# First context tile of a cross-attention kernel in two transfers, with its rounding residues and Gram matrix ordered ahead of the bias rows

## The reference

```
q, k = Wq y + bq, Wk y + bk            (per batch: 128 x 1024)
v    = Wv x + bv
scores = q k^T / sqrt(128)             (within each head: 16 x 16)
out  = softmax(scores) v
o    = Wo out + bo + x
result = (o - mean(o)) / sqrt(var(o) + 1e-5) * gn_w + gn_b    (mean, var over the batch)
```

## Time and profile before

| | us |
|---|---|
| median of 3 executions | 166.63 |
| lowest and highest | 166.38, 167.06 |
| the profiled execution, its own time | 166.47 |
| its span (first to last instruction) | 164.6 |
| PE busy in it | 154.2 (94%) |
| DVE busy | 149.5 (91%) |
| ACT busy | 137.2 (83%) |
| POOL busy | 98.0 (60%) |
| DMA queue of SP, share of 16 engines | 83.3% |

### The profile page before, as it was taken

One profiled execution on the slowest core, in us unless ns is written; L12 is line 12 of the kernel. 1 busy time (PEld: TensorE's weight loads), 2 busy tenths in 40 slices (PEclk: granted clock), 3 DMA queues, 4 the chain that ended last, 5 costly groups with the idle time before them and its releaser, 6 DMA issues. The chain is left out here.

```text
span 164.6 us, 3752 instructions
## 1 busy us (share of the span) xinstructions
PE 154.2 (94%) x932; PEld 121.0 (74%) x932; DVE 149.5 (91%) x686; ACT 137.2 (83%) x354; POOL 98.0 (60%) x162
## 2 busy tenths in 40 slices
PE   7998999999999999999999999999999999998820
PEld 7896887777777788887777777888777777785500
DVE  1788999999999999999999999999999999987861
ACT  3685499999999999999999999999999999767351
POOL 3039267776666676667766666766777666541120
PEclk9999999999999999999999999999999999999995
DMA  5999859999999999998999999999999977631136
GB/s 188 403 407 412 313 196 330 324 338 296 350 342 348 346 357 396 345 336 272 380 377 354 336 344 351 358 334 339 329 374 338 377 308 263 255 127 59 75 127 255
DMA packets 14277, 50.84 MB, mean 309 GB/s; under 512 B 1712, under 2 KB 1712, under 8 KB 14256
## 3 DMA queue, kind: packets, MB, share of 16 engines
q1 hardware_dynamic: 13824, 50.08, 83.3%
q10 hardware_dynamic: 432, 0.53, 0.9%
HBM read 33.82 MB, written 16.78 MB: 307 GB/s over the span
## 5 line engine op out<-in xcount | busy, mean ns | idle before, releaser
L751 PE MATMUL o_ps<-x_sb,m_sb 128*128 128x512 f32 x124 | 61.1, 612 | 0.7 <-ACT out_sb L404 0.7
L751 PE MATMUL g_ps<-hl_sb 128*128 128x258 f32 x256 | 47.0, 308 | 0.0
L484 DVE TENSOR_TENSOR hl_sb<-y_sb,hl_sb 128x512 fp32r<-128x512 f32 x64 | 43.7, 687 | 0.0
L574 DVE BATCH_NORM_STATS2 bn<-o_ps 128x6 f32<-128x512 f32 x62 | 40.3, 685 | 1.4 <-PE o_ps L751 1.4
L325 ACT CAST hl_sb<-y_sb 128x512 fp32r<-128x512 f32 x64 | 39.2, 618 | 1.9 <-DMA y_sb<-in_ctx_dram 1.9
L404 ACT ACTIVATE out_sb<-o_ps,shift,gain 128x1024 f32<-128x1024 f32 x31 | 37.4, 1206 | 2.6
L252 POOL TENSOR_TENSOR lsuma<-hl_sb 128x256 f32<-128x256 f32 x30 | 21.9, 729 | 25.9 <-DVE hl_sb L484 25.9
L751 PEld LDWEIGHTS g_ps<-hl_sb 128*128 128x128 f32 x256 | 35.5, 194 | 0.2 <-DVE hl_sb L484 0.2
L263 POOL TENSOR_TENSOR lsumb<-hl_sb 128x256 f32<-128x256 f32 x30 | 21.9, 729 | 17.5 <-DVE hl_sb L484 17.5
L751 PEld LDWEIGHTS o_ps<-x_sb,m_sb 128*128 128x128 f32 x124 | 21.0, 191 | 14.7 <-issue 14.7
L274 POOL TENSOR_TENSOR lsum<-lsuma,lsumb 128x256 f32<-128x256 f32 x30 | 22.3, 743 | 4.2 <-issue 0.4
(11 more groups left out here) (76 smaller groups left out, 288.9 us busy)
## 6 DMA issues: line engine op xcount, KB each, us to landing
y_sb<-in_ctx_dram SPq DMA_DIRECT2D x32, 512.0 KB, 6.3
x_sb<-in_x_dram SPq DMA_DIRECT2D x32, 512.0 KB, 7.1
out_dram<-out_sb SPq DMA_DIRECT2D x31, 512.0 KB, 6.3
w_in<-in_weights_dram ACTq DMA_DIRECT2D x1, 256.0 KB, 5.4
out_dram<-out_sb ACTq DMA_DIRECT2D x1, 256.0 KB, 2.6
out_dram<-out_sb SPq DMA_DIRECT2D x1, 256.0 KB, 2.8
cols<-in_columns_dram ACTq DMA_DIRECT2D x1, 3.0 KB, 3.4
```

The source lines that it names most:

```text
L484: nc.vector.tensor_tensor(hl_sb[:, b % SLOTS, chunks, C:2 * C], y_sb[:, b % SLOTS, chunks, :], hl_sb[:, b % SLOTS, chunks, 0:C].bitcast(F3 ...
L574: nc.vector.bn_stats(bn[:, b % 2, half, :], o_half(b, half)).then_inc(bn_done, 1)
L751: return nc.tensor.matmul(dst, lhsT, rhs, start=start, stop=stop, **more)
```

## The change

The load of context tile 0 becomes two transfers, one of its first four chunks (signalled by a new semaphore `y_first`) and one of the other four (`y_in[0]`); `round_half(0, 0)` and `round_half(0, 1)` wait for one each. DVE takes both residues of batch 0 before the diagonals. PE takes the Gram matrix of batch 0 before the product that makes the bias rows. ACT's `bias_rows` moves behind `round_half(1, 0)` and `copy_cross(0)`. On DVE `scale_wq` moves behind `rest_half(1, 0)` and `mask_and_bias` behind `rest_half(1, 1)`. What is computed stays the same, and so does the number of instructions, but for one more transfer.

```diff
--- before.py
+++ after.py
@@ -106,6 +106,7 @@
 
 
         y_in = [sem(f"y_in{k}") for k in range(SLOTS)]
+        y_first = sem("y_first")
         x_in = [sem(f"x_in{k}") for k in range(SLOTS)]
         out_done = [sem(f"out_done{k}") for k in range(SLOTS)]
         w_loaded = sem("w_loaded")
@@ -189,6 +190,12 @@
                 if b >= SLOTS:
 
                     sp.wait_ge(l_ready, 2 * (b - SLOTS + 1))
+                tile_y = yT[bass.ds(b, 1)].rearrange("a (p j) c -> p (a j c)", p=P)
+                if b == 0:
+
+                    sp.dma_start(y_sb[:, 0, 0:HCH, :].rearrange("p j c -> p (j c)"), tile_y[:, 0:HCH * C]).then_inc(y_first, 16)
+                    sp.dma_start(y_sb[:, 0, HCH:CH, :].rearrange("p j c -> p (j c)"), tile_y[:, HCH * C:CH * C]).then_inc(y_in[0], 16)
+                    return
                 sp.dma_start(y_sb[:, b % SLOTS, :, :].rearrange("p j c -> p (j c)"),
                              yT[bass.ds(b, 1)].rearrange("a (p j) c -> p (a j c)", p=P)).then_inc(y_in[b % SLOTS], 16)
 
@@ -316,7 +323,12 @@
             def round_half(b, half):
                 if not live(b):
                     return
-                if half == 0:
+                if b == 0:
+                    if half == 0:
+                        act.wait_ge(y_first, 16)
+                    else:
+                        act.wait_ge(y_in[0], 16)
+                elif half == 0:
                     act.wait_ge(y_in[b % SLOTS], loads(b))
                     if b >= SLOTS:
 
@@ -406,9 +418,9 @@
 
             round_half(0, 0)
             round_half(0, 1)
-            bias_rows()
             round_half(1, 0)
             copy_cross(0)
+            bias_rows()
             round_half(1, 1)
             round_half(2, 0)
             round_half(2, 1)
@@ -471,11 +483,6 @@
             dve.wait_ge(const_pool, 6)
             nc.vector.tensor_copy(ident_r[:, :], ident[:, 0:P]).then_inc(const_dve, 1)
 
-            dve.wait_ge(c_loaded, 16)
-            nc.vector.tensor_scalar(diag[:, 0, :], ident[:, 0:P], bq_raw, SCALE * E, ALU.mult, ALU.mult).then_inc(const_dve, 1)
-            nc.vector.tensor_scalar(diag[:, 1, :], ident[:, 0:P], bk_raw, -float(E), ALU.mult, ALU.mult).then_inc(const_dve, 1)
-            nc.vector.tensor_scalar(bq_col[:, :], bq_raw, -SCALE * L, None, ALU.mult).then_inc(const_dve, 1)
-
             def rest_half(b, half):
                 if not live(b):
                     return
@@ -483,6 +490,12 @@
                 dve.wait_ge(h_ready, 2 * b + 1 + half)
                 nc.vector.tensor_tensor(hl_sb[:, b % SLOTS, chunks, C:2 * C], y_sb[:, b % SLOTS, chunks, :],
                                         hl_sb[:, b % SLOTS, chunks, 0:C].bitcast(F32), ALU.subtract).then_inc(l_ready, 1)
+
+            def bias_diagonals():
+                dve.wait_ge(c_loaded, 16)
+                nc.vector.tensor_scalar(diag[:, 0, :], ident[:, 0:P], bq_raw, SCALE * E, ALU.mult, ALU.mult).then_inc(const_dve, 1)
+                nc.vector.tensor_scalar(diag[:, 1, :], ident[:, 0:P], bk_raw, -float(E), ALU.mult, ALU.mult).then_inc(const_dve, 1)
+                nc.vector.tensor_scalar(bq_col[:, :], bq_raw, -SCALE * L, None, ALU.mult).then_inc(const_dve, 1)
 
             def scale_wq():
                 dve.wait_ge(w_loaded, 16)
@@ -644,12 +657,13 @@
 
             rest_half(0, 0)
             rest_half(0, 1)
+            bias_diagonals()
+            rest_half(1, 0)
             scale_wq()
-            mask_and_bias()
-            rest_half(1, 0)
             add_gram(0)
             copy_high_sum(0)
             rest_half(1, 1)
+            mask_and_bias()
             copy_sum(0)
             add_query_bias(0)
             rest_half(2, 0)
@@ -854,12 +868,13 @@
             pe.wait_ge(const_dve, 1)
             keep_busy(WARM_UP)
 
+            pe.wait_ge(const_dve, 4)
+            gram(0, 0)
+            gram(0, 1)
+
             pe.wait_ge(const_dve, 6)
             product(row_ps[:, :, :].rearrange("p v e -> p (v e)"), onesn[:, :],
                     diag[:, :, :].rearrange("p v e -> p (v e)")).then_inc(rows_ready, 1)
-
-            gram(0, 0)
-            gram(0, 1)
             low_sum(0, range(0, HCH))
             transpose_cross(0)
             low_sum(0, range(HCH, CH))
```

## The result

The changed kernel takes 168.59 us in the median of ten executions (167.50 to 171.22), against 166.63 (166.28 to 167.06) before: a ratio of 1.0118, with a 95% interval of 1.0096 to 1.0140. The ten times stand in groups: 167.50, 167.53, 167.76, 167.89, 167.90, then 169.27, 169.49, 169.51, 169.72, and one of 171.22. Those of before have no groups. The profiled execution took 169.49, so it belongs to the upper one; its span is 167.3.

What follows compares the result with a forecast made beforehand. PE bounds the loop, so only the first matmul on x can move: 0.7 us gained at the Gram matrix, given back at the bias rows, `copy_sum(0)` +0.12, taken as +0.15, for a median of 166.8 us (165.9 to 167.5).

Steps and rivals of the forecast that it cites:

- the moment to watch: Start of `copy_sum(0)` on DVE, 9.04 before and 9.16 forecast; its shift goes through to the first matmul on x.
- The bias rows: Behind batch 0's Gram products on PE, ready at 7.3; ACT's copies wait for them, giving back the 0.7 us gain.
- The third rival: The split brings nothing: both halves of tile 0 land by 4.1, `copy_sum(0)` at 9.5, +0.47, 167.1 us; chance 0.10.
- first step: the loads: Tile 0's first half lands at 3.5, second at about 4.15, tile 1 at 6.2, tile 2 unchanged at 7.5.
- the order of issue: Loads land in the order issued, the weights ahead of tile 1; the sum is then +0.15 us.
- the second half lands late: Tile 0's second half lands at 6.6, `copy_sum(0)` at 10.9, +1.9, 168.5 us; chance 0.05.
- the rule: DMA engines take queues in turn, so the weights push tile 0's second half to 4.8; sum +0.35 us.
- second step: the clock: PE's matmul pace doubles at 6.75 as before, with bias rows then ready at 7.3.
- The two long instructions of DVE: Batch 3's residues and `pivot_column` shorten with another timing, 0.3 plus 0.5 us, giving 166.0; chance 0.13.
- the coincidence with POOL: Possible cause of DVE's two long instructions: a coincidence of times with POOL or the loads, which another timing may avoid.
- The gain: Rival: the earlier Gram matrix of batch 0 reaches the end, up to 0.7 us remaining, 165.9; chance 0.12.

Runs made afterwards that it cites:

- the late places: Bias copies behind batch 1's second rounding, `mask_and_bias` behind batch 2's residues: 166.53 us from the filled order alone (167.06), 167.35 from the filled kernel (167.85).
- the filled order alone: Changed kernel without the split of tile 0 (one transfer, new orders kept), with ten warm-up products on PE in place of eight: 167.06 us, ratio 1.0028.
- the filled kernel: Changed kernel with nine warm-up products in place of eight and two unused ones between the halves of batch 0's Gram matrix: 167.85 us, ratio 1.0063.
- the other pair: `late_rows_split` against the filled order alone with the same late places: 167.35 against 166.53 us, on one chip.
- the kernel with a gap: Kernel before the change with six warm-up products in place of eight, so PE idles early: 167.23 to 173.53 us over seven executions, ratio 1.0078.
- late_rows_split: The filled kernel with ACT's bias copies behind batch 1's second rounding and `mask_and_bias` behind batch 2's residues: 167.35 us, ratio 1.0053.

## Why the prediction was wrong

**Right.** PE bounds the loop, and only the start of the first matmul on x moves. `copy_sum(0)` is the moment to watch: in the eight profiles without a late rise or a fall of the clock that matmul starts 6.38 to 6.47 behind it, whatever the order and the loads. The first Gram product started at 4.99 (forecast 4.85), the first rounding at 3.50. The bias rows are what ACT waits for next (8.94 after 8.09), and `mask_and_bias` stands ahead of `copy_sum(0)` without cover; the late places for both gave back 0.2 to 0.4. The third rival put the new order with a whole tile 0 at +0.47, and the filled order alone measured +0.5.

**Wrong, first step: the loads.** "The second half should be in at about 4.15", and tile 1 at 6.2, by the order of issue at an unchanged rate. They landed at 5.4 and 7.05 (over the profiles of kernels split in this way, 4.4 to 5.4 and 6.75 to 7.5). I moved bytes in my account and left the rate at the 256 KB per 0.7 us of the kernel before; with both halves on SP's queue it was 253 and 279 GB/s where it had been 374 and 408. The rival "the second half lands late" named the place and said that it decides from 4.35 on; I gave it 0.05. Its 168.5 lies next to the measured 168.59, but by luck: it is worked out for a landing at 6.6 and has no clock in it. Without the upper group this step costs 0.6 to 0.8 in the time (two pairs of kernels). The Trainium skill's rule that the engines take the queues in turn ("DMA: Bandwidth & Descriptors", queues, rings and completion order), which I had set aside for the order of issue, fits the second half better: with the weights beside it, it landed at 4.8 to 4.9 in three profiles of five, where I had 4.8 by the rule. It landed at 4.4 and 5.4 in the other two. The rule doesn't give tile 1's landing, nor the drop of the rate, which stays with the weights moved to SP.

**Wrong, second step: the clock.** "If the pace doubles at 6.75 as before": I took the moment from the trace and kept it, while the change took away what had been there before it, a PE without a pause. The forecast has the first Gram product right behind the warm-up (4.84 to 4.85) and doesn't ask what a late half does in their middle: PE idled 0.16 and 0.63. From there on until about 13.4 every matmul ran at half the pace. `copy_sum(0)` is 2.0 later and the matmul on x 2.66; in the filled kernel, where tile 1 is as late (7.1), both are 0.64 later (9.68 and 16.06). The two groups of the changed kernel lie 1.75 apart, and filling PE removes the upper one.

**Sum.** Order 0.5 and split 0.6 make the 1.1 of the filled kernel, and of the lower group; with the 0.8 of the other pair it is 1.3. With the upper group, +2.9 in about half the executions, the median comes to +2.0.

**The rivals.** The two long instructions of DVE partly vanished: `pivot_column` took 0.26 at 17.52 and the two residues 1.55 at 15.62, in place of 0.70 and 1.82. That is 0.7 less in this execution; no run shows how much of it reached the end. In both profiles `pivot_column` ends within 0.02 of the POOL instruction beside it (15.12 and 15.11 before, 17.78 and 17.76 with the change), which speaks for the coincidence with POOL that I had named, without showing it. The gain got through nowhere: where the Gram matrix was early, the rows, the tile or the weights were not.

**Open.** What makes tile 1 late and lowers the rate. Rows of 2 KB and the weights on the other queue are not needed, and the number of first transfers alone doesn't do it (it didn't with the second half on ACT). A further transfer on SP's queue ahead of tile 1 goes with it every time, be it only 3 KB; whether by the transfer or by tile 1's later issue, and through what in the DMA engines, no run here tells. Nor is it told why one execution of four with the 3 KB took 166.65, or why the lower group of the kernel with a gap stands 0.8 above the kernel before. No profile caught the changed kernel's lower group, so that its clock rises early is concluded from the filled kernels.

## What to carry to other kernels

Before the head of a kernel is reordered, write down for each microsecond of it whether TensorE has work, and keep it at work up to the point where the loads arrive: pauses of 0.16 and 0.63 us, before the pace of the matmuls had doubled, went with 1.75 us in half the executions, and a few unused matmuls removed that. Splitting a first load brings its first part early (3.5 in place of 4.1) but may delay all that comes behind it, so it is to be judged by the landing of the next two tiles. An instruction that sits in another wait is free only there: `mask_and_bias` and two copies of 0.27, moved out of the way again, were worth 0.2 to 0.4.

## What the runs showed that I had not expected

- A transfer of 3 KB more, ahead of tile 1 on SP's queue, took a kernel of 166.5 us to 171.2 in three executions of four, through a tile that landed 2 us later, a pause of 1.38 us of TensorE, and a granted clock of 0.50 afterwards.
- The clock rises at quite different times, by the pace of the matmuls: in the profile of the changed kernel after 13 (the Gram products from 11.33 on at 0.21 each), in that of its filled form before 5 (0.72 for four at 4.93), in that of `late_rows_split`, filled too, between 5 and 6.7 (1.20 for the first four, 0.73 for the others).
- The clock column showed 1.00 at the start of the kernel before, while the matmuls ran at half the pace, and in the changed kernel up to 13. A fall later on it did show (0.50). The distance between like matmuls tells the pace in both cases.
- A 512 KB tile split by partitions, both halves with full rows, made the kernel before 3% slower, the worst of all forms tried: PE waited 2.56 for the second half, and the clock then fell.
